# Second attention: exponential ahead of the transposed copies, scores and maxima two units ahead

## The reference, cut to what matters

```python
q = layernorm(x) @ Wq; k = ctx @ Wk; v = ctx @ Wv            # 16 heads of 64
scores = einsum('bhsd,bhkd->bhsk', q, k) / sqrt(64)           # (2, 16, 512, 1024)
out = einsum('bhsk,bhkd->bhsd', softmax(scores), v)
x = x + tanh(g_xattn[1]) * (out @ Wo + bo)
```

## Time and profile before

| what | value |
|---|---|
| time, median of 3 runs | 1268.04 us (1263.68 to 1269.64) |
| the profiled execution, own time | 1265.38 us |
| its span in the trace | 1263.6 us |
| mean granted TensorE clock | 0.962 |
| second attention, first to last maximum (L1278) | 455.2 to 999.9 us |

### The profile page before, as it was taken

The page is one execution under the profiler, slowest core; times in us unless marked ns, Lnnn a source line. Parts: engine busy times, 40 slices in busy tenths (PEclk is TensorE's granted clock), DMA queues, the critical chain, the costliest instruction groups (busy, mean ns, idle before and its releaser), DMA issues. The chain is left out here.

```text
span 1263.6 us, 20142 instructions
## 1 busy us (share of the span) xinstructions
PE 1097.2 (87%) x6824; PEld 954.5 (76%) x6824; DVE 898.9 (71%) x1517; ACT 679.8 (54%) x1237; POOL 278.6 (22%) x280
## 2 busy tenths in 40 slices
PE   1869987996699659899898989899997988999998
PEld 1758876885488548788787878788886877888887
DVE  6689838898733648787777778787878866555555
ACT  3467756773211447676675767677777732323222
POOL 5050005003511030402012030402020032344432
PEclk9889989999699979999999999999999988999999
DMA  4000000003101000000100010000000003444332
GB/s 148 1 5 1 1 1 1 2 1 110 27 16 38 1 1 1 2 1 3 36 1 2 1 36 2 1 1 1 27 1 1 1 26 86 112 116 115 103 101 80
DMA packets 18046, 38.20 MB, mean 30 GB/s; under 512 B 3776, under 2 KB 10048, under 8 KB 17440
## 3 DMA queue, kind: packets, MB, share of 16 engines
q1 hardware_dynamic: 17952, 37.01, 10.0%
HBM read 35.76 MB, written 1.25 MB: 29 GB/s over the span
## 5 line engine op out<-in xcount | busy, mean ns | idle before, releaser
L270 PE MATMUL PS<-R 128*128 128x512 f32 (+2 forms) x2728 | 644.1, 381 | 67.6 <-POOL R L424 15.2
L270 PEld LDWEIGHTS PS<-R 128*128 128x128 f32 x2728 | 461.6, 197 | 145.5 <-issue 42.5
L1289 DVE TENSOR_TENSOR R<-PS,R 128x512 fp32r<-128x512 f32 x352 | 225.5, 686 | 62.5 <-ACT R L1022 57.3
L1022 ACT ACTIVATE R<-PS 128x512 fp32r<-128x512 f32 x352 | 190.0, 596 | 146.9 <-PE PS L608 146.8
L608 PE MATMUL PS<-eye,FA 128*128 128x128 f32 x1408 | 188.5, 279 | 40.7 <-ACT FA L998 31.2
L608 PEld LDWEIGHTS PS<-eye,FA 128*128 128x128 f32 x1408 | 155.0, 141 | 74.7 <-issue 26.3
L619 PEld LDWEIGHTS PS<-R 128*128 128x128 f32 x1408 | 186.0, 189 | 26.4 <-issue 11.7
L619 PE MATMUL PS<-R 128*128 128x256 f32 x1408 | 193.4, 283 | 8.6 <-DVE FB L1297 8.3
L998 ACT ACTIVATE FA<-PS,nmax 128x1024 f32<-128x1024 f32 (+1 forms) x160 | 193.0, 1206 | 3.4 <-DVE nmax L1278 3.4
L1278 DVE TENSOR_REDUCE nmax<-PS 128x1 f32<-128x1024 f32 x128 | 155.6, 1216 | 16.6 <-PE PS L270 11.5
L424 POOL TENSOR_SCALAR R<-R 64x512 fp32r<-64x512 f32 x40 | 26.1, 654 | 432.9 <-ACT R L1139 371.0
(11 more groups left out here) (159 smaller groups left out, 1038.2 us busy)
## 6 DMA issues: line engine op xcount, KB each, us to landing
FB<-comb SPq DMA_DIRECT2D x48, 256.0 KB, 3.8
wst<-we_in SPq DMA_DIRECT2D x26, 384.0 KB, 4.0
wst<-w_in SPq DMA_DIRECT2D x4, 1024.0 KB, 5.0
wst<-w_in SPq DMA_DIRECT2D x3, 512.0 KB, 6.3
x<-x_in SPq DMA_DIRECT2D x2, 512.0 KB, 5.7
FB<-ctxT_in SPq DMA_DIRECT2D x2, 512.0 KB, 4.6
FB<-k_in SPq DMA_DIRECT2D x8, 128.0 KB, 2.4
FB<-ctxT_in SPq DMA_DIRECT2D x4, 256.0 KB, 3.9
```

What stands on the lines that cost most here:

```text
L270: last = mm(out, a, b, start=(n == 0), stop=(n == len(passes) - 1), skip_group_check=skip)
L1022: a_(L.pt[0][:, (u // 2) % 2, 4 * g_:4 * g_ + 4, (u % 2) * P:(u % 2) * P + P], L.turn(u, g_).rearrange("p (t n) -> p t n", t=4), ACT.Copy) ...
L1289: inc(v.tensor_tensor(lo, turned, hi.bitcast(F32), ALU.subtract), "p_lo")
```

## The change

```diff
--- before.py
+++ after.py
@@ -634,18 +634,20 @@
                         scores(L, C, u, n)
             first(pe, "x_att", 2 * C - 1)
             for u in range(UNITS + 2):
+                if L.layer == 1 and u + 2 == UNITS // 2:
+                    pe.wait_ge(s["k_lo"], 4 * (C - 1))
+                if L.layer == 1 and u + 2 < UNITS:
+                    scores(L, C, u + 2, 0)
+                    scores(L, C, u + 2, 1)
                 if u < UNITS:
                     for g_ in range(L.ng):
                         turn(u, g_)
                 if L.layer == 0 and u + 2 == UNITS // 2:
                     pe.wait_ge(s["qk0_lo"], 8 * b + 8)
                     pe.wait_ge(s["qk0_lo_pool"], 8 * b + 8)
-                if L.layer == 1 and u + 2 == UNITS // 2:
-                    pe.wait_ge(s["k_lo"], 4 * (C - 1))
                 if u + 2 < UNITS:
-                    scores(L, C, u + 2, 0)
-                    if L.layer == 1:
-                        scores(L, C, u + 2, 1)
+                    if L.layer == 0:
+                        scores(L, C, u + 2, 0)
                 elif filler:
                     filler(u)
                 if u == 2:
@@ -853,12 +855,12 @@
 
                 def next_projections(u):
 
-                    if u < UNITS - 1 or u > UNITS:
+                    if u < UNITS - 2 or u > UNITS - 1:
                         return
-                    if u == UNITS - 1 and b == 1:
+                    if u == UNITS - 2 and b == 1:
                         pe.wait_ge(s["w1q_split"], g_ + 2)
-                    pe.wait_ge(s["expd"], UNITS * C + u)
-                    project(1 - b, J1, range(2) if u == UNITS - 1 else range(2, 4))
+                    pe.wait_ge(s["expd"], UNITS * C + u + 1)
+                    project(1 - b, J1, range(2) if u == UNITS - 2 else range(2, 4))
 
                 attention(L1, b, C, next_projections if nxt else None)
                 if nxt:
@@ -1011,6 +1013,8 @@
             if L.layer == 0:
                 exp(L, C, 0)
             for u in range(UNITS + 3):
+                if L.layer == 1 and u + 1 < UNITS:
+                    exp(L, C, u + 1)
                 if u >= 4 and u % 2 == 0:
                     out_copy(u // 2 - 2)
                 if u < UNITS:
@@ -1021,7 +1025,7 @@
                             first(act, "pv_done", K0 + u // 2 - 1)
                         a_(L.pt[0][:, (u // 2) % 2, 4 * g_:4 * g_ + 4, (u % 2) * P:(u % 2) * P + P],
                            L.turn(u, g_).rearrange("p (t n) -> p t n", t=4), ACT.Copy).then_inc(s["p_hi"], 1)
-                if u + 1 < UNITS:
+                if L.layer == 0 and u + 1 < UNITS:
                     exp(L, C, u + 1)
                 if filler:
                     filler(u)
@@ -1154,7 +1158,7 @@
                 J1 = 28 * g_ + 14 * (b + 1)
 
                 def next_projections(u):
-                    project_hi(C + 1, J1, {UNITS: range(2), UNITS + 1: range(2, 4)}.get(u, ()))
+                    project_hi(C + 1, J1, {UNITS - 1: range(2), UNITS: range(2, 4)}.get(u, ()))
 
                 def next_norm(u):
                     if u == 2:
@@ -1309,11 +1313,11 @@
                         last = v.tensor_copy(dst, src.unsqueeze(3).to_broadcast([P, 2, 2, DH]))
                     inc(last, "rspread")
 
-            if L.layer == 0:
-                maximum(L, C, 0)
+            ahead = 1 + L.layer
+            maximum(L, C, L.layer)
             for u in range(UNITS + 3):
-                if u + 1 < UNITS:
-                    maximum(L, C, u + 1)
+                if u + ahead < UNITS:
+                    maximum(L, C, u + ahead)
                 if u >= 4 and u % 2 == 0:
                     out_sum(u // 2 - 2)
                 if u < UNITS:
@@ -1516,7 +1520,7 @@
                 J1 = 28 * g_ + 14 * (b + 1)
 
                 def next_projections(u):
-                    project_lo(J1, {UNITS: range(2), UNITS + 1: range(2, 4)}.get(u, ()))
+                    project_lo(J1, {UNITS - 1: range(2), UNITS: range(2, 4)}.get(u, ()))
 
                 def next_norm(u):
```

## The result

The changed kernel takes 1305.97 us (median of 4 runs, 1302.04 to 1308.07) against 1268.84 us (4 runs, 1263.68 to 1272.48): a ratio of 1.0298, 95% interval 1.0271 to 1.0326, 37 us slower. The profiled execution's own time is 1305.37 us, its span 1303.6 us. The side was forecast, at 1293.4 us with a range of 1276.0 to 1305.0; the measured median lies 1 us above the range, and the slowing is a third larger than the 28 us forecast. Of the 12.6 us between the median and the forecast, 9.1 are this larger slowing; the other 3.5 are there because the forecast was added to one execution of the kernel before (1265.38 us), and the median of that kernel is 1268.84.

The account below looks back on a forecast made before the run. PE was taken as the busiest engine, held by a loop with ACT 0.26 us per unit above its work. Six inner blocks 24 us, the first 3, the last 1: 28 us over 1265.4 gives 1293.4 us, range 1276 to 1305.

Parts of the forecast that it names:

- The loop of 3.00 us and its 0.26 us above PE's work: Second attention, each unit: ACT and PE wait for each other in turn, 3.00 us, 0.26 above the busiest engine's work.
- The steady wait: Even passes 4 to 12: PE's values wait for the output sum behind the maximum; 1.18 us each, 5.9 per block.
- the 0.10 us for a restart after the wait: Even passes 4 to 12: PE's first matmul after waiting for the output sum costs 0.10 us more.
- The values of pair 7: Block end: PE's values of pair 7 wait for the output sum behind projections 0 and 1; 2.2 us per block.
- Rival B: Block end: later waits absorb the wait of pair 7's values, so it does not show; 1278 us, chance 0.13.
- The start of a block: Block start: PE waits 1.0 us for exponential 1, then transposes 1 and 2 for low copies; together 2.1 us.
- The sum: Second attention, inner block: PE's standing after the change, 10.6 us, less 6.7 before; 3.9 us slower per block.
- rival C: Block ends: the new gap brings one low-clock stretch each, 1.7 us lost, 12 in all; 1305 us, chance 0.08.
- Rival A: Second attention: the gaps close and nothing takes their place; -33 us in all, 1232 us, chance 0.06.

## Why the prediction was right in direction and wrong in size

**The loop of 3.00 us and its 0.26 us above PE's work** were right: with the waits out of the way two units take 5.51 us, 0.49 less than before.

**The steady wait** was right: chain 2.87 us (forecast 2.86), two units 6.67 (6.66). Turning only the order of output sum and maximum round takes 41 us away. One part of it was right by luck: the 0.10 us for a restart after the wait. In the changed kernel a run of 8 lasts 1.20 us without any wait (803.61 above) and 1.21 behind one, so the longer run goes with its new place behind the transposes, not with the wait; PE stands for 1.15 us, not 1.08, since the transposes in front now take 0.79 us in place of 0.85 (796.15 to 796.94 in the same trace), and the values follow 1.94 us after their start (798.90 to 800.84).

**The values of pair 7** were right: 6.15 us after the transposes (6.2), about 2.0 us of standing (2.1). Rival B is out: with the wait gone every block end is 1.2 us shorter at the same clock (20.61 and 21.85), so it had not been absorbed.

**The start of a block** was right in kind and size: 1.03 us before the scores of unit 3 (799.80 + 0.85 to 801.68, and just as much at 842.14 to 844.02 in the changed kernel), forecast 1.0.

**The sum** of 3.9 us per block was right where it can be read without the clock, 3.8 us in block 5. With the clock kept up at the block ends the change costs 30.5 and 29.5 us (1297.46 against 1266.93, 1296.9 against 1267.39); forecast 28. Two more stretches at block starts than before are still in that, about 3 us by an estimate from the 1.55 us each. (As written the terms add up to 27.4, six times 3.9 and 4, and the low end of the range by its own words would be 1271, not 1276. Neither changes the outcome.)

**The step that failed** is the clock: the sum has no term for it, and it was set apart as rival C, "the clock falls (1305 us)", with a chance of 0.08. I had named the mechanism, its place and its price (1.7 us a stretch, 12 in all at seven block ends), but treated it as a thing that would probably not happen, and ended the range on it. Measured are 1.55 us a stretch at five of seven ends, 7.8 us, and 8.5 to 9 us less once the gap is filled; with two more stretches at block starts than before, the clock is about 11 of the 37 us (an estimate, seven times 1.55). It is no rival of the waits: it follows from one of them.

The sentence "no row here shows a gap of 2 us by itself lowering it" was true of the rows printed, but the trace of the kernel before has such gaps. At three block starts PE stands for the same 2.42 us. One of them was followed by the stretch of the earlier trace rows, two were not (the one not shown ends at 527.26), and neither were four other gaps of 1.9 to 2.7 us in the same attention:

```profile
670.27 5.33 PE L270 MATMUL PS<-R 128*128 128x256 f32 x28 [2.42 <-DVE R L1335]
813.87 4.03 PE L270 MATMUL PS<-R 128*128 128x256 f32 x28 [2.42 <-DVE R L1335]
```

The same 28 matmuls take 1.3 us longer in the first. One in seven, or one in three of those at block starts, times seven new gaps at 1.7 us each would have put 2 to 4 us into the sum, as an estimate. So the trace gave reason for a term, but not for the five of seven that came.

A second part of the miss has nothing to do with the mechanism: the 3.5 us between the execution that the sum was added to and the median. I left such an offset (2.7 us then) "in the range", but its upper end, 1305, has no room for it.

The rule of the Trainium skill that I cited with rival C (TensorE: Matmul & The Clock Gate, What's actually happening) is that activity is what releases the throttle. The runs agree with it: the spare matmuls do no useful work, and the program is 9 us shorter.

Rival A did not come out as the change stood. With the output sum, the output copy and the projections moved it came out in part, 20 us of its 33. By the rule of the Trainium skill (Perfetto Trace Analysis, Optimization Strategy) the gaps on the most contended engine are closed by making what they wait for start sooner. Here that found the right gap, and the row behind it told what else had to move.

What stays open is why five of seven block ends have the stretch and two not, with gaps of 1.86 to 1.95 us at all of them. The spread of the runs goes with the mean granted clock as well: of the 13 runs of the kernel before, the fastest had 1263.69 us at 0.965 and the slowest 1273.1 at 0.956, and with the output sum ahead of the maximum 1259.99 us came at 0.963 and 1275.71 at 0.949.

## What to carry to other kernels

When work is moved ahead on one engine, look at what stands behind it in that engine's list: here a maximum moved by one unit took a short output sum with it, which a third engine needed 1 us earlier, and the fix was to swap the two. A wait that shows once per block in a trace, at the one place without cover, is a sign for every place from which the cover is about to be removed; its price there has to be worked out anew (0.2 us before, 1.2 after). Price the clock together with each new gap on TensorE, not as a separate case.

## What was not expected of the hardware

A gap of 2 us on PE at a block end (1.88 in the row) was followed by a stretch at 1.2 GHz in five of seven cases and cost 1.55 us beyond itself, while shorter gaps (0.90 in the row), one in every 6.7 us, left the granted clock at 2.4 GHz. The kernel before shows that such a fall is not certain: of its three gaps of 2.42 us at block starts one was followed by a stretch. Filling the long gap with seven matmuls that nothing reads made the kernel 9 us faster. In the kernel with the maximum one unit ahead, where PE stands up to 2.6 us again and again, the mean granted clock over the span fell to 0.921, from 0.953.
